# Three key tiles added on VectorE instead of two, value steps spread one to a gap, and the gate's bank freed by copies

## The reference, cut to what matters

```
h    = relu(x @ w_down) @ w_up + x                 # w_down, w_up made from cond
sim  = cumprod(agree(paths_q, paths_k)).sum() / 5  # equals phi_q . phi_k, 32 features a head
ctx  = softmax(causal(sim)) @ (h @ Wv)             # 8 heads of 32 channels
x2   = x + ctx @ Wo
y    = x2 @ (U @ V) + bias                         # z = x2 @ U has 30 columns
e    = argmax(y @ gate)                            # 8 experts, first on a tie
out  = y + y @ expert[e].T
```

## Time and profile before

| | us |
|---|---|
| median of 3 runs | 152.74 (152.51 to 153.7) |
| the profiled execution, whole | 153.3 |
| its span in the profile | 151.2 |
| TensorE matmul busy in the span | 141.7 |
| VectorE busy | 87.6 |
| ScalarE busy | 56.4 |
| GpSimd busy | 30.2 |

### The profile page before, as it was taken

One profiled execution on the slowest core, in us unless ns is written; L12 is line 12 of the kernel. 1 busy time (PEld: TensorE's weight loads), 2 busy tenths in 40 slices (PEclk: granted clock), 3 DMA queues, 4 the chain that ended last, 5 costly groups with the idle time before them and its releaser, 6 DMA issues.

```text
span 151.2 us, 5082 instructions
## 1 busy us (share of the span) xinstructions
PE 141.7 (94%) x2294; PEld 89.3 (59%) x2294; DVE 87.6 (58%) x164; ACT 56.4 (37%) x67; POOL 30.2 (20%) x56
## 2 busy tenths in 40 slices
PE   5999679999979979999999999999999999999993
PEld 5646346554645655657566756576567677666651
DVE  0473727866794848387816575549256852975431
ACT  3013370564253225357522461673234447310010
POOL 7200022011042120650112224200222440110000
PEclk9999999999999999999999999999999999999999
DMA  4999999700111000000000000000011010101111
GB/s 109 316 399 424 385 365 351 255 9 0 18 32 21 4 0 4 0 4 4 35 35 4 35 7 4 35 4 32 3 39 39 0 38 1 39 35 39 69 41 69
DMA packets 7381, 12.50 MB, mean 83 GB/s; under 512 B 1552, under 2 KB 5808, under 8 KB 7232
## 3 DMA queue, kind: packets, MB, share of 16 engines
q1 hardware_dynamic: 7120, 11.73, 21.9%
q0 software_dynamic: 96, 0.05, 0.9%
q10 hardware_dynamic: 144, 0.39, 0.6%
HBM read 9.95 MB, written 2.22 MB: 81 GB/s over the span
## 4 chain that ended last, share of the span: by engine, by line
PE 84%; DVE 11%; issue 2%; ACT 1%; POOL 0%; POOLq 0%; ACTq 0%; DVEq 0%
PE work L588 39%; PE c_ps L588 23%; PE s_ps L588 16%; PE work L767 3%; DVE rden L440 2%; PE work L707 2%; DVE h_t L473 1%; ACT prob L387 1%; DVE feat L578 1%; DVE u_w L514 1%; DVE phi_t L490 1%; PE work L759 1%; DVE w_up L466 1%; DVE x_t L566 1%; DVE q_bd L495 0%
## 5 line engine op out<-in xcount | busy, mean ns | idle before, releaser
L387 ACT ACTIVATE prob<-s_ps 128x1536 f32<-128x1536 f32 (+1 forms) x24 | 38.3, 1594 | 43.5 <-PE s_ps L588 43.4
L440 DVE RECIPROCAL rden<-c_ps 128x256 f32<-128x256 f32 x16 | 28.1, 1758 | 22.7 <-PE c_ps L588 22.7
L364 POOL TENSOR_SCALAR_AFFINE_SELECT prob<-prob 128x1024 f32<-128x1024 f32 x16 | 19.2, 1202 | 90.3 <-ACT prob L387 90.3
L588 PE MATMUL s_ps<-phi_t 32*128 32x256 f32 (+1 forms) x384 | 24.2, 365 | 1.1 <-DVE phi_t L490 0.6
L588 PE MATMUL c_ps<-prob,v_sb 128*32 128x256 f32 (+1 forms) x384 | 24.9, 346 | 0.0
L588 PEld LDWEIGHTS s_ps<-phi_t 32*128 32x128 f32 x384 | 17.4, 184 | 11.1 <-issue 8.5
L588 PE MATMUL work<-ctx_t,mix_sb 128*32 128x256 f32 x256 | 17.0, 381 | 0.4
L588 PE MATMUL work<-zo_t,gexp 128*32 128x256 f32 x256 | 16.9, 379 | 0.0
L588 PEld LDWEIGHTS c_ps<-prob,v_sb 128*32 128x32 f32 x384 | 11.6, 110 | 8.7 <-issue 1.7
L588 PE MATMUL c_ps<-prob,ones 128*32 128x256 f32 (+1 forms) x256 | 16.3, 326 | 0.0
L588 PE MATMUL work<-w_vl,h_t 128*32 128x296 f32 x208 | 14.8, 416 | 0.9 <-DVE pick L551 0.5
(11 more groups left out here) (96 smaller groups left out, 133.3 us busy)
## 6 DMA issues: line engine op xcount, KB each, us to landing
wdec<-in_W_dec SPq DMA_DIRECT2D x1, 3855.0 KB, 18.2
x_t<-in_x_tr SPq DMA_DIRECT2D x4, 512.0 KB, 8.7
ex_t<-in_expert_tr SPq DMA_DIRECT2D x1, 2048.0 KB, 25.2
out_x<-x_t SPq DMA_DIRECT2D x16, 128.0 KB, 1.7
mix_sb<-in_mix SPq DMA_DIRECT2D x1, 776.0 KB, 19.7
lift_sb<-in_lift ACTq DMA_DIRECT2D x1, 384.0 KB, 3.8
w_vl<-in_vl SPq DMA_DIRECT2D x1, 296.0 KB, 5.0
first_sb<-in_first SPq DMA_DIRECT2D x1, 144.0 KB, 3.4
```

Of the source, the lines that this page charges most:

```text
L364: nc.gpsimd.affine_select(out=tri, in_=tri, compare_op=ALU.is_ge, fill=0.0, base=0, pattern=[[0, HG], [0, 2], [1, P]], channel_multiplier= ...
L387: nc.scalar.activation(prob[:, p % 2, :, 0:width(p)], s_ps[:, :, 0:width(p)], ACT.Exp).then_inc(exped, 1)
L440: link(nc.vector.reciprocal(rden[:], c_ps[m % 2][:, CW:2 * CW]))
L588: return nc.tensor.matmul(o, w, r, start=start, stop=stop, skip_group_check=True)
```

## The change

- `long(p)` takes the place of `opening(p)`: each pair of a long chunk now has an `add`, but for the last pair of all (p = 23). In the closing pair VectorE adds key tile 2, once masked, to `tiles`; the `ones` matmuls over that tile go, and those over `tiles` move from the start of `context` to its end.
- In batches 1 and 2 the value steps stand one to a gap: VL 0 before context 1, VL 1 behind it (and behind out 3), VL 2 before context 2, VL 3 behind it, straight before the features.
- `zs` copies the scores to a new tile `score`; the two copies free the bank, the five operations read `score`, and `zo` waits on a new semaphore `picked`.

```diff
+def long(p):
+    return pair(p)[1][1] == 1 and p < ALL - 1
 def adds(p):
-    return sum(opening(i) for i in range(p + 1))
+    return sum(long(i) for i in range(p + 1))
...
-        gaps[1] += [("zs", prv, ALL_T), ("zo", prv, 0), ("zo", prv, 1), ("VL", n1, 0), ("VL", n1, 1)]
-        gaps[2] += [("VL", n1, 2), ("VL", n1, 3)]
+        gaps[1] += [("zs", prv, ALL_T), ("zo", prv, 0), ("zo", prv, 1), ("VL", n1, 0)]
+        gaps[2] += [("VL", n1, 2)]
...
-    if b >= 1 and n1 < B:
-        gaps[2] += features(n1, ALL_T)
     if prv >= 1:
         gaps[1] += [("out", prv - 1, 3)]
+    if b >= 1 and n1 < B:
+        gaps[1] += [("VL", n1, 1)]
+        gaps[2] += [("VL", n1, 3), *features(n1, ALL_T)]
...
-        if _p + 1 < ALL and opening(_p + 1):
+        if _p + 1 < ALL and long(_p + 1):
             ORDER += [("add", _p + 1)]
...
-                    done(pool, ("zs", b, ALL_T))
+                    pool.wait_ge(picked, b + 1)
...
-                        if opening(p - 2):
+                        if long(p - 2):
                             act.wait_ge(added, adds(p - 2))
...
+                    acc = tiles[:, chunk(p) % 2]
                     dve.wait_ge(exped, p + 1)
-                    nc.vector.tensor_tensor(tiles[:, chunk(p) % 2], both[:, :, 0, :], both[:, :, 1, :], ALU.add
-                                            ).then_inc(added, 1)
+                    if opening(p):
+                        nc.vector.tensor_tensor(acc, both[:, :, 0, :], both[:, :, 1, :], ALU.add).then_inc(added, 1)
+                    else:
+                        dve.wait_ge(masked, masks(p))
+                        dve.wait_ge(added, adds(p) - 1)
+                        nc.vector.tensor_tensor(acc, acc, both[:, :, 0, :], ALU.add).then_inc(added, 1)
...
-                    sc = bank(s)[:, P:P + nt * E].rearrange("p (t e) -> p t e", e=E)
+                    sc = score[:, span]
...
+                    nc.vector.tensor_copy(sc.rearrange("p t e -> p (t e)"), bank(s)[:, P:P + nt * E]
+                                          ).then_inc(empty(s), 1)
+                    done(dve, s)
...
-                                            ALU.is_equal).then_inc(empty(s), 1)
+                                            ALU.is_equal).then_inc(picked, 1)
...
-                if half and last:
-                    pe.wait_ge(added, adds(p))
-                    for h in range(HG):
-
-                        mm(c_ps[m % 2][DH * h:DH * (h + 1), CW:2 * CW], ones[:], tiles[:, m % 2, h, :],
-                           start=False, stop=False)
...
-                    if half and first:
+                    if half and (first or i == 0 and p < ALL - 1):
                         continue
...
+                if half and last:
+                    pe.wait_ge(added, adds(p))
+                    for h in range(HG):
+
+                        ins = mm(c_ps[m % 2][DH * h:DH * (h + 1), CW:2 * CW], ones[:], tiles[:, m % 2, h, :],
+                                 start=False, stop=True)
```

More of the change, by code:

```diff
@@ L247, in build @@
         kmax = sb("kmax", [P, TT])
+        score = sb("score", [P, TT, E])
         hit = sb("hit", [P, TT, E])
@@ L282, in build @@
         u_ready = sem("u_ready")
+        picked = sem("picked")
         zo_ready = sem("zo_ready")
@@ L552, in _ @@
                                             kmax[:, span].unsqueeze(2).broadcast_to([P, nt, E]),
-                                            ALU.is_equal).then_inc(empty(s), 1)
+                                            ALU.is_equal).then_inc(picked, 1)
                 elif kind == "zo" and s[1] == B - 1:
                     _, b, hf = s
-                    done(dve, ("zs", b, SECOND if hf else FIRST))
+                    dve.wait_ge(picked, B + hf)
                     for t in (2 * hf, 2 * hf + 1):
@@ L643, in context @@
                         ins = mm(c_ps[m % 2][DH * h:DH * (h + 1), CW + lo:CW + lo + n], ones[:],
-                                 prob[:, p % 2, h, CW * i:CW * i + n], start=False, stop=(last and i == 1))
+                                 prob[:, p % 2, h, CW * i:CW * i + n], start=False, stop=(not half and i == 1))
+                if half and last:
[3 more added lines that the diff above has]
+                                 start=False, stop=True)
                 ins.then_inc(summed, 1)
```

## The result

The changed kernel took 153.72 us (median of 22 runs, 153.15 to 154.5) against 152.93 us for the kernel before, measured beside it 22 times. The ratio is 1.0052, with a 95% interval of 1.0032 to 1.0072: slower by 0.8 us. I had forecast +0.65 us.

The account below looks back on a forecast made before the run. TensorE's queue, matmuls busy 94% of the span, was taken to set the time nearly everywhere. Terms 1.44 - 0.86 - 0.43 + 0.30 + 0.20 = +0.65 on 152.74 gave 153.4 us, 8-in-10 range 151.9 to 154.7.

Parts of the forecast that it names:

- Pairs 9 and 15: First closing pairs of batches 1 and 2: TensorE waits 1.5 to 1.8 for the add; each stage 0.72 us longer.
- T: End of the last value step, 97.15 in batch 2 before the change; forecast to move by +0.44.
- The stalls for `pick`: Value steps of batches 1 and 2: the stall before VL 1 goes, gaining about 0.42 us in each.
- Pairs 11 and 17: Second closing pairs of batches 1 and 2: the add ends just before it is wanted; 2 x 0.43 = -0.86 us.
- Pair 21: Closing pair in batch 3: the add ends at about 125.8, before TensorE wants the sum; -0.43 us.
- Batch 0: Closing pairs 3 and 5: the first add delays the reciprocal by 0.29, the second's saving is lost; +0.30 us.
- Tail: Kernel's end, through the last `zs` and `zo` to `zoT`: the copy of scores adds 0.20 us.
- The lock: Slower rival: a GpSimd mask over bias, features or add at pairs 9 and 15 lengthens the wait; 154.7 us, chance 0.12.

Follow-up runs that it names:

- all three edits: Changed kernel with pairs 9 and 15's add before the features, no third tile in batch 0, ScalarE's `zo` copies before the exponential: 150.37 us, 0.9846.
- The second experiment: Kernel before with only the third tile's new adds, value steps and bank as they were: 153.62 us, ratio 1.0024.

## Why the prediction was right

By its own steps:

- **Pairs 9 and 15**, the place that I said decides: forecast +0.72 a stage, measured +0.69 and +0.69, with the holes at 1.36 and 1.37 where "1.5 to 1.8" was forecast. The bracket was 0.1 too high at its lower end: I counted from when the last group could be followed (T + 2.95), and the profile counts idle time from that group's modelled end (101.26, T + 3.05). The sum wasn't touched by it. That the add behind the features is the cause is shown by moving it alone (0.9887), and its price by the half and the full extra add (waits +0.6 and +1.14) and by the 1.56 that are gone with all three edits.
- **The stalls for `pick`**: gone, as forecast, and worth 0.5 to 0.6 us with the tail's 0.2 taken off (0.9968 and 0.9961). What I put down to VL 1's new place belongs to the copies alone.
- **Pairs 11 and 17**: forecast -0.43 with less than 0.1 to spare; -0.42 and -0.41 measured, 0.06 to spare in pair 17.
- **Pair 21**: the matmuls went as forecast (-0.42), but 0.20 came back one step later. `out` 0 of batch 3 waits for a bank that ScalarE's first copy of `zo` frees, and that copy stands behind an exponential of 1.88. Here the changed kernel's TensorE:

```profile
127.46 0.61 PE L604 MATMUL c_ps<-tiles,ones 128*32 128x256 f32 x8
128.09 1.07 PE L604 MATMUL work<-ctx_t,mix_sb 128*32 128x256 f32 x16
```

  and its ScalarE:

```profile
125.68 1.88 ACT L395 ACTIVATE prob<-s_ps 128x2048 f32<-128x2048 f32 x1 [0.73 <-PE s_ps L604]
127.45 1.07 ACT L430 COPY zo_t<-work 128x512 f32<-128x512 f32 x2
```

  The two copies take 1.07, so the first ends near 128.0, and TensorE starts at 128.09. I had asked what is late next only of VectorE.
- **Batch 0**: forecast +0.30, measured +0.15. The term was mis-sized: the reciprocal moved by 0.20 and not 0.29, and 0.05 came back later. That pair 5 gains nothing was right.
- **Tail**: forecast +0.20, measured +0.22. I wrote that the chain before passes through the arg max; it runs on TensorE's `out` step there, but `zo` ended only 0.15 before `zoT` started in both kernels, so the copy's 0.2 counted in full.
- **The lock**: it did not strike. The mask of pair 9 took 1.10 and ended at 66.43, the bias began at 67.30, 0.87 later. The second experiment, where the two overlap, has the price at 0.65. The mask kept its 1.10 with little room: the opening pair's add ended at 65.29 and the mask began at 65.33. With 1.92 it would, by an estimate from these rows, have ended at 67.25, still just ahead of the bias. The Trainium skill, page "SBUF — State Buffer", section "Who interferes with whom", says that such a conflict matters only where two operations overlap in time; the traces agree.

The sum was +0.65 against +0.79 by the medians and +0.85 in the profiled executions, of which 0.18 come before any changed code. That leaves +0.67 for the change, closer to +0.65 than the terms deserve: two of them were off by -0.15 and +0.20 and nearly cancel, which is luck.

## What to carry to other kernels

Work that is moved from the bound engine to an idle one is free only if its place in that engine's queue is early enough: ask what stands ahead of it and what that waits for, for each place where the pattern repeats. Here the same add was hidden in three places, held TensorE up by 1.56 in two, and in the two of batch 0 it gained nothing. Then ask which third engine is late next: here the hole that closed showed one of 0.37 behind it, for another engine.

## What was not expected of the hardware

Two idle stretches of TensorE of 1.96 us were each followed by some 3.4 us at a granted clock of 0.50 in one profiled execution; three more of that kernel's seven had the same mean clock, 0.978, and the other three stayed at 1.00. Of two stretches of 2.50 us in another kernel one was followed by it; the mean clock was 0.989 in all five of its executions, which fits one such stretch in each. Holes of 1.37 left it at 1.00 in 22 of 22. Where the lower level came, it cost 1.56 to 1.69 us, more than the 0.6 or 1.14 by which the extra add had lengthened the wait. What decides whether a given hole does this stays open here; the two kernels also ran on different chips, so a difference between chips isn't excluded.
